# Other sizes for the seven slots of maxima of an attention stage, and its first corner tables asked for behind the first head's keys

## What is computed

```python
qkv = (x @ qkv_w + qkv_b).reshape(Bw, Nw, 3, nh, dh)
q, k, v = (qkv[:, :, 0], qkv[:, :, 1], qkv[:, :, 2])
attn = jnp.einsum('bnhd,bmhd->bhnm', q * scale, k)
attn = jax.nn.softmax(attn + bias[None], axis=-1)
out = jnp.einsum('bhnm,bmhd->bnhd', attn, v).reshape(Bw, Nw, Cd)
```

## Time and profile before

| what | before |
|---|---|
| median of 3 runs | 6252.09 us (6249.62 to 6258.36) |
| the profiled execution's own time | 6254.11 us |
| its span, first to last instruction | 6252.1 us |
| mean granted TensorE clock | 0.978 |
| TensorE matmul (PE) busy | 94% |
| VectorE (DVE), GpSimd (POOL), ScalarE (ACT) busy | 70%, 69%, 52% |

### The profile page before, as it was taken

How to read it: one execution, slowest core, us unless ns; L and a number is a source line. 1 busy time by engine, 2 the same in 40 slices (tenths; PEclk the granted TensorE clock), 3 DMA queues, 4 the chain that set the end, 5 groups by cost and what they waited for, 6 DMA issues and landing times. The chain is left out here.

```text
span 6252.1 us, 121385 instructions
## 1 busy us (share of the span) xinstructions
PE 5853.5 (94%) x37810; PEld 3448.2 (55%) x37810; DVE 4373.6 (70%) x8484; ACT 3276.0 (52%) x6740; POOL 4323.8 (69%) x1447
## 2 busy tenths in 40 slices
PE   1888888699999999999999999999999999986899
PEld 1666666455555555555555555555555555533566
DVE  1666666587777787777777777777777777736540
ACT  0444444246666666666666666666666666641222
POOL 0333333368888888888888888888888888864453
PEclk9999999889999999999999999999999999997999
DMA  2222222411001101101110110110011000014432
GB/s 46 76 92 90 93 88 92 122 32 33 27 25 36 35 16 36 32 27 25 38 40 18 33 41 21 36 33 27 25 36 35 16 17 17 15 55 129 115 93 46
DMA packets 199805, 297.69 MB, mean 48 GB/s; under 512 B 40436, under 2 KB 164614, under 8 KB 196230
## 3 DMA queue, kind: packets, MB, share of 16 engines
q1 hardware_dynamic: 184206, 269.32, 15.2%
q0 software_dynamic: 12432, 19.38, 1.5%
q10 hardware_dynamic: 2664, 2.62, 0.2%
HBM read 166.35 MB, written 124.51 MB: 47 GB/s over the span
## 5 line engine op out<-in xcount | busy, mean ns | idle before, releaser
L1274 DVE TENSOR_REDUCE tops<-ps_m 128x1 f32<-128x448 f32 (+1 forms) x5600 | 3120.0, 617 | 906.6 <-PE ps_m L1177 856.9
L1250 ACT ACTIVATE prob<-ps_s 128x448 f32<-128x448 f32 (+1 forms) x5600 | 2613.3, 548 | 1749.5 <-PE ps_s L1113 1710.4
L1083 POOL TENSOR_TENSOR tile_sum<-prob 128x1792 f32<-128x1792 f32 x448 | 1803.0, 4025 | 658.3 <-ACT prob L1250 658.1
L1113 PE MATMUL ps_s<-queries,keys 97*128 97x448 f32 (+1 forms) x5600 | 2197.3, 397 | 13.7 <-ACT prob L1250 7.6
L1177 PE MATMUL ps_m<-keys,queries 96*128 96x448 f32 (+1 forms) x5600 | 2090.5, 380 | 35.9 <-DMA keys<-k_parts 20.6
L1083 POOL TENSOR_TENSOR tile_sum<-tile_sum,prob 128x1792 f32<-128x1792 f32 x448 | 1807.4, 4034 | 31.8
L1113 PEld LDWEIGHTS ps_s<-queries,keys 97*128 97x128 f32 (+1 forms) x5600 | 1041.6, 187 | 1154.6 <-ACT prob L1250 660.4
L1129 PE MATMUL ps_o<-prob,values 128*32 128x448 f32 x11200 | 1342.0, 551 | 3.0 <-ACT prob L1250 1.2
L1177 PEld LDWEIGHTS ps_m<-keys,queries 96*128 96x128 f32 (+1 forms) x5600 | 1061.6, 190 | 241.9 <-DVE tops L1274 85.6
L324 POOL TENSOR_TENSOR logit<-logit,top 112x896 f32<-112x896 f32 x112 | 194.6, 1738 | 462.1 <-DVE top L581 462.1
L1129 PEld LDWEIGHTS ps_o<-prob,values 128*32 128x32 f32 x11200 | 226.5, 108 | 379.4 <-issue 244.3
(11 more groups left out here) (182 smaller groups left out, 4171.2 us busy)
## 6 DMA issues: line engine op xcount, KB each, us to landing
queries<-q_parts SPq DMA_DIRECT2D x288, 160.0 KB, 3.3
keys<-k_parts SPq DMA_DIRECT2D x96, 392.0 KB, 7.2
xT<-in_x SPq DMA_DIRECT2D x56, 224.0 KB, 3.1
hidden<-h SPq DMA_DIRECT2D x28, 448.0 KB, 3.3
q_parts<-hi SPq DMA_DIRECT2D x56, 224.0 KB, 1.9
q_parts<-lo SPq DMA_DIRECT2D x56, 224.0 KB, 1.9
k_parts<-hi SPq DMA_DIRECT2D x56, 224.0 KB, 1.9
k_parts<-lo SPq DMA_DIRECT2D x56, 224.0 KB, 1.9
```

What stands on the lines that cost most here:

```text
L1083: nc.gpsimd.tensor_tensor(tile_sum[k % 2][:, :, :], left, prob[:, t % SLOTS, :, :], ALU.add).then_inc(summed, 1)
L1113: mm = nc.tensor.matmul(o[:, 0:CH], keys[x.u][:, j, at:at + k], queries[x.v][:, j, own:own + CH], start=True, stop=not last, skip_group_ch ...
L1250: nc.scalar.activation(prob[0:k, t % SLOTS, j, :], ps_s[0:k, score_bank(x.hm, i), 0:CH], ACT.Exp).then_inc(exp_done, 1)
L1274: nc.vector.tensor_reduce(tops[0:rows, j, r - blocks[0], c:c + 1], ps_m[0:rows, e % MB, 0:CH], AX.X, ALU.max).then_inc(m_used, 1)
```

## The change

Two edits. The list of spills is another one, and with it the sizes of the seven slots. At the start of the stage the corner tables are asked for behind the keys of the first head and ahead of those of the other three.

```diff
-SPILLS = [10, 22, 10, 22, 10, 22, 16]
+SPILLS = [10, 26, 14, 28, 17, 28, 19]
...
             load_queries(first)
-            for j in range(HG):
+            load_keys(first, 0)
+            load_corner(first)
+            for j in range(1, HG):
                 load_keys(first, j)
-            load_corner(first)
             load_values(first)
```

## The result

The changed kernel takes 6334.29 us (median of 4 runs, 6330.54 to 6337.14), the one before 6250.85 in the runs beside it: a ratio of 1.0132 (95% interval 1.0115 to 1.015), 83 us slower. The forecast was 6294 us, range 6274 to 6322. The direction was right and the time lies 12 us above the range. It lies on rival (c), the clock falling in nearly every wait, which was priced at 6334 and given a chance of 0.09.

A forecast was written before the change was run, and what follows sets the result against it. The attention stage was taken to go at the pace of TensorE's queue. Tables -8, slot sizes -16, wait +60 and clock +6 sum to +42 us, from the median of 6252.1 to 6294 us; range 6274 to 6322.

The forecast's parts named there:

- rival (c): TensorE's clock falls in nearly every query-tile wait of halves 3 and 5: 46 us in place of 6, 6334 us; chance 0.09.
- the clock: TensorE's granted clock halves after idle waits, 2.9 us a fall: two falls in eight phases, +6 us, between 0 and +23.
- The wait: TensorE stands for the query tile in halves 1, 3 and 5: 2.2, 3.0, 2.3 us; 60 us for eight phases.
- (a): The query-tile wait costs nothing, because the tile is there in time or the stage has slack: 6228 us; chance 0.06.
- (b): Two thirds of the query-tile wait is taken up by VectorE and ScalarE starting with empty queues: 6248 us; chance 0.05.
- The slot sizes: New entry counts in the attention stage's halves gain 2.4 us a phase; -16 us together, bounds -8 and -21.
- The lower bound of the prediction: Slot sizes by straight lines through the halves: -1.2 us a phase, -8 us together.
- The lag: In groups of five entries without `total`, VectorE is behind: five maxima of 617 ns take 3.09 us.
- The other bound: Slot sizes with every extra entry in a `total` group free: -3.0 us a phase, -21 us.
- the last phase's +1.0: Slot sizes in the last phase, where halves 5 and 6 carry little: a loss of 1.0 us.
- The corner tables: In the prologue the tables land behind the first head's keys, last head starts at 1226.1 instead of 1234.14: gain 8.0 us.

The follow-up runs named there:

- the busy wait: Changed kernel with 9, 13 and 10 overwritten matmuls put ahead of the query tile's wait in halves 1, 3 and 5: 6306.63 us, ratio 1.0086.
- spills less 4: Changed kernel with every spill smaller by 4, same slot sizes, at least 4 maxima of the older query tile at each slot's start: 6236.48 us, ratio 0.9974.
- the slots alone: Kernel before with the new spills only, corner tables in the old order: 6348.32 us, ratio 1.015.
- spills less 3: Changed kernel with every spill smaller by 3, same slot sizes, 3 older maxima at the start of slots 4 and 6: 6262.52 us, ratio 1.0018.

## Why the prediction was wrong

**The step that failed is the clock.** The prediction put it as "two falls in eight phases, +6 us; between none (0) and all eight of half 3 (+23)". The record of the changed kernel has 21 falls at its 24 waits, all eight of half 3, six of half 5 and seven of half 1. They cost 45 us by what comes behind the awaited entries, and 28 to 38 by the plain differences to the busy wait, whose own waits are 6 us longer. Wait and clock together are 98 us where I had 66, and the wait is within 1 us of the 60 that I had; so the 32 us, and by the traces up to 39, are the clock. The forecast as a whole was 40 us low; the rest is the sizes. What misled me was the choice between two cases. I read the earlier trace rows as if the 2.2 us of one idle time were safe and the 2.7 of another were not, with one case of each. In the changed kernel the waits of half 1 and half 5 left PE idle for 1.7 to 2.4 us (once 1.2), and the clock was low at 13 of the 16 (two of them beside the idle time at the end of the loop). Two samples were no ground for taking those halves out of the high end of the range. That rival (c) has the measured time to the microsecond is in part luck: it had 106 us of wait and clock and 16 gained by the sizes, where 98 and 7 were measured, and it left out half 1, where seven of the 21 falls are. The sentence on the Trainium skill (TensorE: Matmul & The Clock Gate, Part 1), that the array goes to half its clock after it has been idle, pointed the right way, and the trace agrees: 0.52 in the first group of half 3 with PE idle for 3.05 us before.

**The wait was right.** Place, count and cause were as told: halves 1, 3 and 5, 24 times. The forecast was 2.2, 3.0 and 2.3 us. Against the run with spills less 4 the awaited entry of the changed kernel comes 2.0, 3.1 and 2.3 us later, as a mean over the phases; together 60 forecast and 59 measured. The landing that the forecast took for half 3 (third DMA, 2.9 us after issue) is 3.1 us in half 38 of the changed kernel. Rivals (a) and (b), that the stage has slack, are out.

**The slot sizes were right in sign and too large.** A fifth entry was put at 0.49 us without `total` and 0.21 with one, and it costs 0.47 in both. So a phase gained 1.5 us by the run with spills less 4 and not 2.4, 11 us in seven phases where the term had 17; of runs against each other, 6243.69 and 6236.48, it is 7 us in place of 16. The lower bound of the prediction (1.2 us a phase, by straight lines through the halves) was the better number, though the lines themselves have the bend at the wrong place. The lag was also overstated: 617 ns is the mean length of records of VectorE that overlap, and by the same line of the earlier trace rows 3120.0 us of busy time for 5600 maxima are 557 ns each, so 2.8 us for five and not 3.09. That is still more than the 2.73 us of a group with four entries, but it leaves 0.7 us over in a group with `total` (3.49), and the fifth entry costs its 0.47 there too. A reading that fits, and that no run has tested by itself, is that this slack stands behind the group's entries, where it can't help the bank that the next entry waits for. The other bound, -21, leaves out the last phase's +1.0; that moves the range by 1 us.

**The corner tables were right.** 8.0 us forecast, 8.2 measured alone, last head at 1225.67 with 1226.1 forecast. The sum by what was measured is -8 for the tables, -7 for the sizes and +98 for wait and clock: 83 us, as the runs of the changed kernel say.

## What to carry to other kernels

When work that was kept in store is moved to level the load, ask which transfer the store was hiding: here four entries of about 0.4 us each kept a load of 3 us from being seen, because the fifth stands behind a burst of other work. TensorE, which was busy all the time in this stage, paid twice for most idle times of 2 to 3 us, once for the wait and once for the matmuls behind it at half the clock, so price both at every place where such a wait comes. And a bound for how often the clock falls needs more than one case of each kind.

## What the runs showed of the hardware

The granted clock fell from 1.00 to 0.50 at idle times of TensorE that were shorter than I had thought. At idle times of 1.7 to 2.4 us (halves 1 and 5 of the changed kernel, the two beside the end of the loop left out) it was low 11 times of 14, at 2.7 to 3.1 us (half 3) 8 of 8; the slots alone gave the same two counts. With the idle time cut to 0.9 to 2.0 us by busy matmuls it was low 4 times of 21, with spills less 3, at 1.0 to 1.9 us, 5 of 10, and with 1.2 us at most (the busy wait) 0 of 23. Idle times between these ends went either way: behind 1.2 us the clock fell once (spills less 3, half 5), and at 2.6 us, at the end of the code's loop in the same run, it stayed at 1.00. At the end of the last phase two idle times of 1.1 and 1.2 us stand close together in all eleven traces, and the clock fell behind them in three. So the length of the idle time does not decide alone. What else decides was not tried.
